# A fused decoder stack on one core: the first bias of the expert pages folded into their matrices, one register load for four pages, and a layer's inputs and gathers issued at other places

## The reference, cut to what matters

```python
x = x + tanh(g_xattn[0]) * L0_xattn(layernorm(x), ctx);   x = x + tanh(g_ffn[0]) * L0_ffn(layernorm(x))   # fp4-rounded linear
x = x + tanh(g_xattn[1]) * L1_xattn(layernorm(x), ctx);   x = x + tanh(g_ffn[1]) * L1_ffn(layernorm(x))
... # L2: perceiver attention, then attention and 8 experts; L3: attention, then 64 experts
```

```python
h = einsum('td,edf->etf', xt, W1) + b1[:, None, :]      # 128 -> 512
h = _layernorm(jax.nn.relu(h), g1, be1)
y = einsum('etf,efd->etd', h, W2) + b2[:, None, :]      # 512 -> 128
y = _layernorm(jax.nn.relu(y), g2, be2)
out = einsum('te,etd->td', gate, y)                     # gate: 2 of 8 experts
```

## Time and profile before

| what | value |
|---|---|
| median of 3 runs | 1967.96 us (1967.61 to 1969.69) |
| the profiled execution: its own time, its span | 1967.84 us, 1965.9 us |
| busy over the span | PE 86%, PEld 57%, DVE 59%, ACT 42%, POOL 38% |
| block 2 (107.2 to 233.2 us): busy PE / DVE / POOL | 69.6 / 73.1 / 52.0 of 126 us |
| block 3 (233.2 to 468.0 us): busy PE / DVE / ACT / POOL | 144.7 / 106.2 / 109.9 / 65.7 of 234.8 us |

### The profile page before, as it was taken

One profiled execution on the slowest core, in us unless ns is written; L12 is line 12 of the kernel. 1 busy time (PEld: TensorE's weight loads), 2 busy tenths in 40 slices (PEclk: granted clock), 3 DMA queues, 4 the chain that ended last, 5 costly groups with the idle time before them and its releaser, 6 DMA issues. The chain is left out here.

```text
span 1965.9 us, 31203 instructions
## 1 busy us (share of the span) xinstructions
PE 1691.6 (86%) x10277; PEld 1121.0 (57%) x10277; DVE 1166.7 (59%) x3013; ACT 821.1 (42%) x2113; POOL 739.2 (38%) x964
## 2 busy tenths in 40 slices
PE   6745686655999999999999997969999899999999
PEld 5534464443566555765567655445765565655656
DVE  6846454544775756757567575466757655554655
ACT  2310254642554555635556354315645522222222
POOL 3424314144664744647446474004647400000000
PEclk8865788978999999999999998989999999999999
DMA  8020111111000000000000000000000273734452
GB/s 290 1 69 22 52 32 51 33 35 35 3 1 1 1 2 1 1 1 2 2 1 2 1 1 2 0 1 1 1 2 1 75 211 115 210 117 123 134 163 86
DMA packets 63838, 92.51 MB, mean 47 GB/s; under 512 B 11072, under 2 KB 29120, under 8 KB 62912
## 3 DMA queue, kind: packets, MB, share of 16 engines
q1 hardware_dynamic: 61632, 86.32, 14.3%
q0 software_dynamic: 2048, 4.20, 0.7%
HBM read 80.53 MB, written 9.96 MB: 46 GB/s over the span
## 5 line engine op out<-in xcount | busy, mean ns | idle before, releaser
L1563 POOL TENSOR_TENSOR rows<-rows,rinv 128x512 f32<-128x512 f32 x192 | 198.2, 1060 | 144.5 <-DVE rinv L1799 144.5
L2470 ACT ACTIVATE region_b<-psum 128x512 f32<-128x512 f32 x132 | 78.8, 597 | 258.0 <-PE psum L2432 257.9
L1725 ACT ACTIVATE rows<-psum,nmax 128x512 f32<-128x512 f32 x192 | 130.1, 684 | 124.8 <-DVE nmax L1792 124.7
L2508 DVE TENSOR_TENSOR region_b<-region_b,psum 128x512 f32<-128x512 f32 x128 | 87.9, 686 | 128.4 <-ACT region_b L2470 126.0
L2444 PEld LDWEIGHTS psum<-region_c,region_b 128*128 128x128 f32 x1024 | 132.1, 192 | 56.1 <-issue 43.7
L1791 DVE TENSOR_REDUCE lg<-psum 128x2 f32<-128x1024 f32 x128 | 155.7, 1216 | 5.7 <-PE psum L1609 2.3
L1908 POOL TENSOR_TENSOR rows<-rows,rinv 128x128 f32<-128x128 f32 (+2 forms) x192 | 127.1, 684 | 75.5 <-DVE rinv L2077 75.5
L1803 DVE COPY turned<-psum 128x512 f32<-128x512 f32 x128 | 88.4, 690 | 92.3 <-PE psum L1621 91.9
L2072 DVE TENSOR_REDUCE nmax<-psum 128x1 f32<-128x128 f32 (+3 forms) x256 | 113.7, 486 | 40.8 <-PE psum L1954 39.8
L1609 PE MATMUL psum<-region_a,region_b 64*128 64x256 f32 x1024 | 132.2, 397 | 2.9 <-ACT rows L1725 2.9
L2444 PE MATMUL psum<-region_c,region_b 128*128 128x128 f32 x1024 | 133.4, 275 | 1.5 <-DVE region_b L2516 1.5
(11 more groups left out here) (740 smaller groups left out, 3632.1 us busy)
## 6 DMA issues: line engine op xcount, KB each, us to landing
pt<-gates SPq DMA_DIRECT2D x128, 128.0 KB, 3.1
ysb<-gates SPq DMA_DIRECT2D x128, 128.0 KB, 3.6
region_a<-in_eg SPq DMA_DIRECT2D x32, 256.0 KB, 3.4
region_a<-in_eu SPq DMA_DIRECT2D x32, 256.0 KB, 3.5
region_c<-in_weights SPq DMA_DIRECT2D x32, 256.0 KB, 4.7
sorted<-kctx SPq DMA_DIRECT2D x2, 1536.0 KB, 14.2
turned<-sorted SPq DMA_DIRECT2D x12, 256.0 KB, 3.1
made<-rows SPq DMA_DIRECT2D x12, 256.0 KB, 3.4
```

The costliest lines, as they stand in the source:

```text
L1563: nc.gpsimd.tensor_tensor(row(u, j), row(u, j), rinv[:, 2 * u + j:2 * u + j + 1].broadcast_to([P, S]), ALU.mult).then_inc(s.pn, 1)
L1725: nc.scalar.activation(row(u, j), s_bank(u, j), ACT.Exp, bias=nmax[:, 2 * u + j:2 * u + j + 1], accum_out=sum_column(u // T, u % T, j)).th ...
```

## The change

1. **The bias folded.** A new side of block 2, `fold_b1`, replaces each expert's first matrix W by W minus its column means plus b1/128 in every row: for each expert PE multiplies `centre` (identity minus 1/128) with W, adds eight rows of b1/128 picked by a broadcast column of the identity, and ACT copies the sum back. POOL makes `centre` and b1/128 first. The page's rows get 1 added when they are copied out of PSUM (`copy_rows`: Identity with bias 1). Since a row x sums to zero, (x+1) times the new matrix is xW + b1. `add_bias` and its register load go, and so does the load of `b1_rows`.
2. **Relu from PSUM.** ACT takes relu directly from the product's bank; its order in a step is relu(k), copy of page k-1, square(k). DVE takes over every fourth `copy_hidden` (page 3 of a quad), POOL the relu of the quad's result.
3. **One register load for a quad on DVE.** `route_1` packs the owners of four pages as octal digits of one integer (`owner_quad`); DVE loads it once for a quad and computes the offsets from it.
4. **Three buffers instead of two** for the loaded rows and the results, with semaphores by thirds. PE's `value_load` stands before its waits. DVE's and POOL's orders within a quad change; `rows_stats` moves one step later.
5. **Loads.** Block 2 issues the fronts' ten inputs before it clears semaphores; `be2_rows` is loaded after they have landed; and its SP stream ends by loading quads 0 to 2 of the pages, so block 3 finds them there.
6. **Gathers.** The gathers of step 40 have a buffer of their own and no longer wait. The 16 gathers of block 4 are spread, two before each of POOL's steps 1 to 8; DVE adds them in steps 6 and 10.

```diff
@@ copy_rows, scalar
-                    nc.scalar.activation(page_t[:, q % 2, :], bank(0), ACT.Copy).then_inc(s.xtc, 1)
+                    nc.scalar.activation(page_t[:, q % 2, :], bank(0), ACT.Identity, bias=one_col[:, 0:1]).then_inc(s.xtc, 1)
@@ pages_1, scalar
                 for k in range(n_pages + 9):
                     if k == 0:
                         copy_rows(0)
-                    if 1 <= k <= n_pages:
+                    if k < n_pages:
+                        relu(k)
+                    if 1 <= k <= n_pages and not on_dve(k - 1):
                         copy_hidden(k - 1)
-                    if k < n_pages:
-                        relu_and_square(k)
                     if k % 4 == 1 and k // 4 + 1 < n_quads:
                         copy_rows(k // 4 + 1)
-                    if k >= 7 and k % 4 == 3 and k // 4 - 1 < n_quads:
-                        relu_rows(k // 4 - 1)
+                    if k < n_pages:
+                        square(k)
                     yield k
@@ pages_1, vector
-                def add_bias(k):
...
-                    at_row = owner(nc.vector, owner_512, k, F1)
-                    nc.vector.tensor_tensor(hid[:, k % 2, :], up_bank(k), region_b[:, bass.ds(at_row, F1)],
-                                            ALU.add).then_inc(s.hb, 1)
+                def at_row(q, j):
+                    return bass.ds((of_quad[q] // 8 ** j) % 8 * D, D)
+
+                def copy_hidden(k):
+                    dve.wait_ge(s.th, k + 1)
+                    dve.wait_ge(s.dn, k - 1)
+                    nc.vector.tensor_copy(hid_t[:, k % 2, :], turn_bank(k)).then_inc(s.thc_dve, 1)
...
+                for k in range(n_pages + 8):
                     q = k // 4 - 1
+                    if k % 4 == 0:
+                        if 0 <= q < n_quads:
+                            copy_hidden(k - 1)
+                        if 0 <= q - 1 < n_quads:
+                            rows_stats(q - 1)
+                    if k % 4 == 1 and 0 <= q < n_quads:
+                        if q == QUADS:
+                            group_ready(dve, "owner")
+                        of_quad[q] = nc.vector.value_load(owner_quad[0:1, q // QUADS, q % QUADS:q % QUADS + 1])
+                        hidden_var(q)
+                    if k % 4 == 2 and 0 <= q < n_quads:
+                        rows_bias(q)
+                    if k % 4 == 3 and 0 <= q - 1 < n_quads:
                         rows_centre(q - 1)
                         rows_add(q - 1)
@@ pages_1, gpsimd
-                for k in range(n_pages + 9):
+                for k in range(n_pages + 8):
                     q = k // 4 - 1
...
+                    if k % 4 == 1 and 0 <= q - 1 < n_quads:
...
+                        rstd_link(nc.gpsimd.tensor_scalar(w.rstd2[:, :], w.mv[:, :, 1], LN_EPS, None, ALU.add))
+                        rstd_link(nc.gpsimd.tensor_tensor(w.rstd[:, :], w.rstd2[:, :], neg_half[:, :], ALU.pow))
+                    if k % 4 == 1 and 0 <= q < n_quads:
+                        pool.wait_ge(s.hv, q + 1)
...
+                        nc.gpsimd.tensor_tensor(hrs[:, :], rtmp[:, :], neg_half[:, :], ALU.pow).then_inc(s.hrstd, 1)
+                    if k % 4 == 3 and 0 <= q < n_quads:
+                        pool.wait_ge(s.yb, 4 * (q + 1))
+                        nc.gpsimd.tensor_scalar(page_y[q % 3], page_y[q % 3], 0.0, None, ALU.max).then_inc(s.yrelu, 1)
                     yield k
@@ fold_b1, tensor and scalar
+                for e in range(E8):
+                    yield e - 4
+                    if e == 0:
+                        pe.wait_ge(s.f_ready, 2)
+                    if e >= 4:
+                        pe.wait_ge(s.f_taken, e - 3)
+                    nc.tensor.matmul(into(e), centre[:, :], w1[:, e, 0:F1], start=True, stop=False)
+                    nc.tensor.matmul(into(e), ident[0:E8, e:e + 1].broadcast_to([E8, P]), b1[:, :], start=False,
+                                     stop=True).then_inc(s.f_made, 1)
...
+                    nc.scalar.activation(w1[:, e, 0:F1], into(e), ACT.Copy).then_inc(s.f_taken, 1)
@@ attention_2, gpsimd
-                    for batch in late:
-                        batch.gather(pool)
...
                     for n in range(steps):
+                        if late and 1 <= n <= 8:
+                            late[(n - 1) // 4].gather(pool, 2 * ((n - 1) % 4), 2)
                         four = ctx_rows(n)
@@ fronts_beside_route
+            def first_loads(sp):
                 load_inputs(sp, sf, 2, front_1)
                 load_inputs(sp, sg, 3, front_2)
-                lo = early_at["b1"][0]
-                sp.dma_start(b1_rows[:, :, :], over(a["early"][0:E8, lo:lo + F1], 0, [P, E8, F1])).then_inc(sw.tables_in, 16)
+
+            def sync(sp):
+                sp.wait_ge(sf.inputs, 5 * 16)
+                sp.wait_ge(sg.inputs, 5 * 16)
...
                 sp.wait_ge(scattered_1[0], 16 * K1 * GT)
+                for q in range(3):
+                    load_pages(sp, s_pages, q)
```

More of the change, by code:

```diff
@@ L309, in flamingo_kernel @@
                           rstd2=part(region_a, w_at + 40, [P, T]), xn=part(work, 0, [P, T, D]), xnt=part(wide_2, 3584, [P, S]))
-        b1_rows = part(region_b, 0, [P, E8, F1])
+        page_rows = part(region_b, F1, [P, 3, 4, D])
+        page_t = part(region_b, 4 * F1, [P, 2, 4 * P])
+        page_y = [part(rows2, F1 * n, [P, 4, D]) for n in range(3)]
         be2_rows = part(region_c, 0, [P, E8, D])
@@ L335, in flamingo_kernel @@
         lower_r = part(kvt, 2 * P + 8 + PAGES, [P, E8 * E8])
[L336 removed]
+        count_i = part(kvt, 4 * P, [P, E8 + PAGES]).bitcast(I32)
         slots = sb("slots", [P, 2, K1 * GT], I32)
@@ L1151, in gpsimd @@
                 if g == 0:
+                    for j in range(4):
+                        mm = nc.gpsimd.memset(eights_r[:, j:j + 1], float(8 ** j))
+                    mm.then_inc(s.r_iota, 1)
                     nc.gpsimd.iota(count_i[:, 0:E8], [[1, E8]], base=0, channel_multiplier=0).then_inc(s.r_iota, 1)
@@ L1421, in wait_stored, with gather @@
             def wait_stored(eng):
-                eng.wait_ge(s.out_even, 16 * (QUADS // 2))
-                eng.wait_ge(s.out_odd, 16 * (QUADS // 2))
-            def gather(pool):
-                wait_stored(pool)
-                if before is not None:
-                    pool.wait_ge(s.xd, before)
-                for n in range(K1):
-                    for t in range(T):
-                        col = GT * n + T * i + t
-                        nc.gpsimd.indirect_dma_start(found_at[:, n, t, :], None, made_1[g][:, :],
-                                                     bass.IndirectOffsetOnAxis(ap=slots[:, g, col:col + 1], axis=0)).then_inc(found, 16)
+                for stored_third in (s.out_0, s.out_1, s.out_2):
+                    eng.wait_ge(stored_third, 16 * (QUADS // 3))
+            def gather(pool, lo=0, count=K1 * T):
+                if lo == 0:
+                    wait_stored(pool)
+                for n, t in ((m // T, m % T) for m in range(lo, lo + count)):
+                    col = GT * n + T * i + t
+                    nc.gpsimd.indirect_dma_start(found_at[:, n, t, :], None, made_1[g][:, :],
+                                                 bass.IndirectOffsetOnAxis(ap=slots[:, g, col:col + 1], axis=0)).then_inc(found, 16)
             def add(dve):
```

198 lines of the change are left out of this document (97 added, 101 removed).

## The result

The changed kernel takes **1906.2 us** (median of 4, 1903.6 to 1911.1) against 1967.98: a ratio of 0.9687, 95% interval 0.9667 to 0.9708. Forecast were 1912 us and 1890 to 1932. The profiled execution took 1906.4 us, its span is 1904.5.

A forecast was written before the change was run, and what follows sets the result against it. No engine was full in block 3; a chain of waits bound it. Terms -60 (pages), -4.7 (block 3's start), -2.5 (block 2) and +11 (block 4's gathers) made -56, so 1912 us, range 1890 to 1932.

The forecast's parts named there:

- What bounds the pages: Block 3: a chain of waits through DVE's load and add sets the 14.2 us lap; afterwards PE bounds it at 9.6.
- Parts 1 to 4 by stretches: Block 3 from 240.0 to its end, five stretches forecast one by one: 168 us for 228.0, so -60.
- the first stretch: Block 3, 240.0 to 284.9, first pages beside `route_1`: 33 us instead of 44.9.
- The end at 330.0: Block 3: end of the scatters' stretch, taken as the second group's first product; 37 us instead of 45.1 up to it.
- Three buffers don't help here: Block 3's scatters: the third buffer gains nothing, since the load of quad 6 still waits for all scatters.
- The slower rival: Block 3: DVE's register arithmetic costs what a load costs, 16.5 us a quad; about 2024 us in all, chance 0.03.
- The rule against part 2: Block 3: DVE instructions with two SBUF inputs contend with POOL's relu; up to 1.6 us a quad, left out of the sum.
- Part 5: Block 3 starts 4.7 us earlier through preloaded quads; block 2, with earlier loads and the fold, changes by -2.5 us.
- about five of them fit there or nearly: Block 2: about five of the fold's eight experts fit into PE's wait for inputs, which ends at 120.31.
- the second rival: Block 2: the fold runs at the low clock and delays the fronts, +9 instead of -2.5 us; 1920 to 1923, chance 0.07.
- Part 6: Block 4: spread gathers stand in series with POOL's steps 1 to 8, 8.4 us a step instead of 7.04, +11.
- they hide: Block 4 of the kernel before: its 16 gathers, 20.3 us, are hidden beside kv products and the first scores.

The follow-up runs named there:

- e10: The kernel before, with ACT's relu taken directly from PSUM, without DVE's bias add and its register load (b1 left out): 1936.8 us, ratio 0.9787 to the kernel before.
- e8: The changed kernel with the relu of a quad's result moved back from POOL to ACT: 1901.9 us, ratio 0.9611 to the kernel before.
- e2: The changed kernel with the fold's experts 2 to 7 moved to later places in block 2: 1897.7 us, ratio 0.9591 to the kernel before.
- e1: The changed kernel with block 4's 16 gathers issued again ahead of POOL's first step: 1909.0 us, ratio 0.9651 to the kernel before.
- e12: The changed kernel with DVE's adds of gathered rows in block 4 moved from steps 6 and 10 to 10 and 16: 1900.9 us, ratio 0.96.
- e11: The changed kernel with four register loads a quad written on DVE instead of one: 1906.9 us, ratio 0.9632 to the kernel before.
- e3: The changed kernel with DVE's adds of gathered rows in block 3 moved from steps 37 and 44 to 41 and 47, a norm later: 1905.4 us, ratio 0.9627.
- e4: The changed kernel with block 4's gathers ahead, the fold's experts later and block 3's adds later, all together: 1895.6 us, ratio 0.9586 to the kernel before.

## Why the prediction was right, and where it was not

- **What bounds the pages.** Right. The chain through DVE's load and add was what 14.2 us a lap were made of, and PE bounds the lap after it: 9.20 us, all of it busy, where 9.6 was taken from two pages 2.39 us apart. e10 shows that the shorter chain alone leaves 10.6; what brings it to 9.2 wasn't separated. One sign failed: DVE's idle time before the bias was to be under 1 us and is 2.65, a wait for POOL's `hrs`, which costs nothing while PE is never idle. (The row at 347.84 is both passes of the first product and not its last; the end that the prediction works with is right.)
- **Parts 1 to 4 by stretches.** -60 forecast, -69.2 measured; the stretches, with the forecast in brackets: 28.7 (33), then two with together 70.6 (74), 20.6 (21), 39.1 (40). The largest error is the first stretch, where 4 us were added for filling the pipe and for route's own chain; PE idled 0.9 us in it.
- **The scatters and the third buffer.** The end at 330.0 was misread as the second group's first product, so the two stretches around it compare only as a sum. The row there is DVE's bias of quad 3 after 12.16 us of waiting: it overwrites quad 1's result, and SP's store of that result stood behind the load of quad 6, which waits for all scatters. "Three buffers don't help here" was wrong for this wait: in the changed kernel the same bias runs at 294.77, ahead of the store of quad 1 at 298.75, since it now has to await only quad 0's. By the program two buffers would have made it wait for the store; no run has the change with two, so what the third is worth here isn't measured.
- **Register arithmetic.** The slower rival's ground is gone. "No row has such an operation" held for the rows shown and not for the trace: in the kernel before, L1202 has 0.30 us for a load and 0.19 for the arithmetic behind it, so the prediction's load of 0.5 us was both. In the changed kernel (count, then least, median and longest ns of one):

```profile
L1353 DVEq FUSED_REGOPS  x48: 115/152/177, 252.6 to 390.0; - x48
L1369 DVEq FUSED_REGOPS  x48: 57/57/78, 269.8 to 394.4; - x48
L1377 DVEq ALU_OP  x48: 40/40/52, 270.5 to 396.0; - x48
```

  The offsets cost 4 x (0.152 + 0.057 + 0.040) = 1.0 us a quad, where 2.3 was taken and 16.5 feared.
- **The rule against part 2.** The contention is there, the trace agrees with the Trainium skill ("SBUF — State Buffer", "Who interferes with whom"), and is 0.35 us a quad on one line, under a PE that bounds (e8). What the relu on POOL cost stood elsewhere, in POOL's queue: 7.1 us of block 3 (e8), 3.1 through the scatters, which the prediction had in its sum for that stretch, and 4.0 in the stretch of the gathers, which it had not.
- **Part 5.** The block's start was right in kind and 1.6 us too small. The fold is the step that failed: "about five of them fit there or nearly". Three didn't fit. At 2.0 us a product (the sum had 1.8), the first two experts last until 109.46 + 4 x 2.0 = 117.5, and the inputs had landed by 115.22; and the second rival, the fold at the low clock in front of a chain, held with +4.5 for block 2 where -2.5 was forecast and +9 its price. e2 moves it, block 2 gets 4.5 to 7 us shorter, and with 123.6 is where -2.5 had put it. Two of the signs named as wrong came: a pair of products ahead of the fronts took 4.0 us (3.6 was named), and PE waited for DVE's copy of a fourth page.
- **Part 6.** Against the profiled execution of the kernel before it is right in mechanism and size, +9.2 for +11, a step of 8.15 us for 8.4. But the size hangs on "they hide", and that was partly luck: in e10 the unchanged block takes 171.2 us, and in e1, with the gathers back ahead of the block, 171.8, as long as with the gathers spread. On those two chips the gathers ahead of the block cost 8 us by themselves, and spreading them costs nothing against that. DVE's adds, in both kernels and so outside the difference, are 5.7 us of the changed one's block (e12).
- **The sum.** -56 forecast and -61.4 in the traces: block 2 is 7 above its term, the pages 9 below theirs, the block's start and part 6 2 below each. That the total came within 6 us is in part the cancelling of the first two.

## What to carry to other kernels

A chain that visits an engine for a small operation costs the visit, not the operation: fold the operand into a matrix, read PSUM directly, and count the lap anew by each engine's busy time. When an experiment adds work, count it in the trace before its time is read: in e11 the three added loads aren't in it. Work that is moved into idle time must be put behind what the idle time waits for and not ahead of it; 16 gathers, two ahead of each of eight steps, cost 8 us more than one in the wait of each of sixteen. And an in-order queue with long foreign work in it (eight gathers, 10 us) delays everybody who waits for a 1 us result behind it; the wait is then shown on another engine, as DVE's late copy was here, and moving that one gained nothing (e3).

## What was not expected of the hardware

- PE was busy without a break from 109.46 to 149.00, 39.5 us, and its granted clock stayed at 0.50, the level of 1.2 GHz; from 149.00 to 155.00, still without a break, its mean was 0.71; in the pages, with the same share busy, it was at 1.00. Why it stayed low isn't shown. A product with 8 rows of contraction took as long as one with 128, 2.07 and 2.08 us for 512 columns.
- With 16 indirect gathers in flight at the start of block 4, ACT's and DVE's copies out of PSUM stopped for 3 to 6 us at a time, 8 us in all, in e1, e4 and e10, on two chips; in the profiled execution of the kernel before, with the same gathers in the same place, they didn't. The kernel before was 10 to 12 us slower in the experiments' runs than in the result's and the changed kernel 3, and e10, which has that kernel's block 4 unchanged, loses 9.1 us in it: it fits, but no whole kernel before was profiled beside them. What stops the two engines stays open.
- DVE's additions of 128x512 with both inputs in SBUF took 1.41 us beside POOL's multiplications and 0.69 without (e12).
- A register load on DVE took 0.31 us, and the arithmetic on the loaded number 0.04 to 0.15 us an offset (changed kernel).
